# A state-space layer and its FFN on one core: from pairs of units in a loop to one unit a phase, written out

## The reference, cut to what matters

```python
def layer(x, in_proj_w, conv_w, conv_b, x_proj_w, A_log, D, out_proj_w):
    xz = einsum('bld,ed->ble', x, in_proj_w)              # 256 -> 1024
    x_inner, z = split(xz, 2)
    x_conv = silu(causal depthwise conv of x_inner, 4 taps, + conv_b)
    x_dbl = einsum('bld,ed->ble', x_conv, x_proj_w)       # 512 -> 33
    delta, B, C = softplus(x_dbl[..., 0]), x_dbl[..., 1:17], x_dbl[..., 17:]
    A = -exp(A_log)                                       # 16 states
    h = h * exp(delta * A) + x_conv * (delta * B)         # over 2048 steps
    y = (einsum('bdn,bn->bd', h, C) + x_conv * D) * silu(z)
    return einsum('bld,od->blo', y, out_proj_w)           # 512 -> 256
def ffn(x, ...):
    h = butterfly(x @ W_exp + b_exp, up_weights)          # 256 -> 1024
    h = butterfly(gelu(h + up_bias), down_weights)
    return h @ W_con + b_con + down_bias
x = x + layer(layernorm(x), ...)
x = x + ffn(layernorm(x), ...)
```

## Time and profile before

| | |
|---|---|
| median of 3 runs | 630.66 us |
| profiled execution | 632.72 us, span 630.8 us |
| TensorE busy | 560.5 us (89%) |
| VectorE busy | 443.5 us (70%) |
| ScalarE busy | 303.1 us (48%) |
| GpSimd busy | 123.9 us (20%) |
| mean granted TensorE clock | 0.951 |
| instructions in the profile | 8980 |

### The profile page before, as it was taken

One profiled execution on the slowest core, in us unless ns is written; L12 is line 12 of the kernel. 1 busy time (PEld: TensorE's weight loads), 2 busy tenths in 40 slices (PEclk: granted clock), 3 DMA queues, 4 the chain that ended last, 5 costly groups with the idle time before them and its releaser, 6 DMA issues.

```text
span 630.8 us, 8980 instructions
## 1 busy us (share of the span) xinstructions
PE 560.5 (89%) x2996; PEld 436.9 (69%) x2996; DVE 443.5 (70%) x883; ACT 303.1 (48%) x511; POOL 123.9 (20%) x104
## 2 busy tenths in 40 slices
PE   4989776679999997979999989979999988979996
PEld 3747345647899773747899665847899664848895
DVE  5748868876556789877556699887555699977432
ACT  3655739146055766044144866054254865162252
POOL 4213100240012032250021042250020041340010
PEclk9988876899999999979999998979999999979999
DMA  8332020010010100010000000000100000000000
GB/s 239 4 22 4 0 66 2 1 35 2 3 64 2 34 1 2 0 34 0 33 33 0 33 0 0 0 33 0 33 33 0 33 0 0 0 0 2 0 34 34
DMA packets 33067, 12.88 MB, mean 20 GB/s; under 512 B 22003, under 2 KB 32499, under 8 KB 33044
## 3 DMA queue, kind: packets, MB, share of 16 engines
q1 hardware_dynamic: 31444, 9.96, 7.3%
q10 hardware_dynamic: 1600, 2.62, 1.2%
HBM read 8.39 MB, written 4.19 MB: 20 GB/s over the span
## 4 chain that ended last, share of the span: by engine, by line
PE 58%; DVE 23%; ACT 8%; issue 7%; DMA 2%; POOL 1%; DVEq 0%; ACTq 0%; POOLq 0%
PE acc L869 14%; PE wide L858 12%; PE wide L727 8%; DVE xc L1346 6%; PE wide L847 4%; PE wide L829 4%; PE wide L836 4%; PE wide L736 3%; DVE x1b_xn L1255 2%; PE small L717 2%; DVE soft L1385 2%; PE acc L656 1%; PE small L806 1%; DVE diag_sum L1475 1%; PE small L784 1%
## 5 line engine op out<-in xcount | busy, mean ns | idle before, releaser
L1031 ACT ACTIVATE hid_f<-wide,bias_up 128x512 f32<-128x512 f32 x64 | 44.0, 687 | 139.3 <-PE acc L869 127.4
L1346 DVE SCALAR_TENSOR_TENSOR xc<-xi,taps,xc 128x512 f32<-128x512 f32 x96 | 91.0, 958 | 6.5 <-ACT xc L1060 4.2
L1363 DVE TENSOR_TENSOR hid_low<-hid_f,hid_high 128x512 fp32r<-128x512 f32 x64 | 44.3, 692 | 68.8 <-ACT hid_high L1132 68.2
L869 PE MATMUL acc<-w_down_high,hid_high 128*128 128x256 f32 x256 | 73.9, 289 | 1.5 <-DVE hid_low L1363 1.5
L869 PE MATMUL acc<-w_down_low,hid_high 128*128 128x256 f32 x256 | 71.8, 281 | 0.0
L869 PE MATMUL acc<-w_down_high,hid_low 128*128 128x256 f32 x256 | 71.7, 280 | 0.0
L847 PE MATMUL wide<-w_out,yg 128*128 128x256 f32 x256 | 56.9, 380 | 0.0
L537 POOL TENSOR_TENSOR c_place<-xd,row_in_block 128x1024 f32<-128x1024 f32 x8 | 15.5, 1938 | 208.8 <-DVE xd L1374 208.8
L727 PE MATMUL wide<-xnT_high,w_in_high 128*128 128x512 f32 x128 | 54.9, 429 | 0.0
L858 PE MATMUL wide<-xnT_high,w_up_high 128*128 128x512 f32 x128 | 53.4, 417 | 0.0
L869 PEld LDWEIGHTS acc<-w_down_high,hid_high 128*128 128x128 f32 x256 | 48.2, 188 | 6.6 <-DVE hid_low L1363 4.5
(11 more groups left out here) (184 smaller groups left out, 1136.4 us busy)
## 6 DMA issues: line engine op xcount, KB each, us to landing
x_in<-in_L_attn_x_dram SPq DMA_DIRECT2D x8, 512.0 KB, 3.6
out_dram<-x1b_xn SPq DMA_DIRECT2D x8, 512.0 KB, 2.9
xc<-in_L_attn_in_proj_w_dram ACTq DMA_DIRECT2D x2, 512.0 KB, 6.6
xc<-in_L_ffn_W_exp_dram ACTq DMA_DIRECT2D x1, 1024.0 KB, 9.3
low_w<-in_L_ffn_W_con_dram SPq DMA_DIRECT2D x1, 1024.0 KB, 5.6
raw_out<-n_L_attn_out_proj_w_dram ACTq DMA_DIRECT2D x1, 512.0 KB, 10.3
low_w<-in_L_ffn_up_weights_dram SPq DMA_DIRECT2D x14, 4.0 KB
low_w<-_L_ffn_down_weights_dram SPq DMA_DIRECT2D x14, 4.0 KB
```

The lines of the kernel that those rows point to most:

```text
L869: last = pe.matmul(acc[:, c, :], hid[h][:, j % HRING, c * P:(c + 1) * P], w_down[w][:, j, 0:DM], start=j == 0 and c % 2 == 0 and n == 0, s ...
L1031: ins = act.activation(out_ap, in_ap, how.pop("func"), **how)
L1346: ins = dve.scalar_tensor_tensor(xc[b][:, e, :], xi[:, e, tap:tap + TILE], taps[:, e, tap:tap + 1], xc[b][:, e, :], ALU.mult, ALU.add)
L1363: dve.tensor_tensor(hid[1][:, j % HRING, :], hid_f32[:, j % HRING, :], hid[0][:, j % HRING, :].bitcast(F32), ALU.subtract).then_inc(hid_re ...
```

## The change

The loop goes; every engine's program is one sequence of nine phases. Phase u holds the scan of unit u (now numbered 0 to 7, alternating between the sequences), the input projection, convolution and silu of unit u+1, the FFN of unit u-1, and the first norm of unit u+2. With it:

- C is spread by two DMAs through DRAM (`spread_c` on SP: xd out, and back so that each partition has C of its block); `place_c` and the two products go. `diag` has its states innermost, `diagonal_times_c` is one instruction over 1024 elements.
- `x_projection` writes its four products to two halves of the partitions; the sum of the halves is taken in `xd_tokens_first`, now a product with `fold`.
- all four x_tok tiles are copied by ScalarE (two by VectorE before); `silu_z` comes with `silu_x`, behind the gelus of the phase.
- xnT has a buffer for each norm; x is loaded twice (x_ln, x_res); `gate` works in place in xc.
- the FFN weights are finished in phase 1; the DOWN mixing is done at the end of phase 0.
- the instructions that set the semaphores at the start go, and waits before the first use are left out.

```diff
+            def spread_c(u):
+                read(sp, u, "xdtok", 0)
+                wait(sp, c_spread, u, 16, ago=2)
+                sp.dma_start(c_dram[u % BATCH], xd[:, :, 1 + NS:XD]).then_inc(c_out.handle, 16)
+                wait(sp, c_out, u, 16)
+                wait(sp, diag_summed, u, 1, ago=1)
+                sp.dma_start(c_near[:, :, :, :].rearrange("p u c n -> p (u c n)"),
+                             c_dram[u % BATCH].rearrange("(j u) c n -> j (u c n)", u=BL).unsqueeze(1)
+                             .to_broadcast([NB, BL, BL * GR * NS])).then_inc(c_spread.handle, 16)
...
+            for u in range(1, UNITS):                    # SP
+                load_for_residual(u)
+                if u + 2 < UNITS:
+                    load_for_norm(u + 2)
+                spread_c(u)
+                store(u - 1)
...
+            for u in range(UNITS):                       # GpSimd
+                weigh_gaps(u)
+                mask_b(u)
+                diagonal_gaps(u)
+                place_c_block(u)
+                diagonal_times_b(u)
+                if u:
+                    residual_with_bias(u - 1)
+                if u + 2 < UNITS:
+                    rstd_of(u + 2, 0, var1, rstd1)
+                rstd_of(u, 1, var2, rstd2)
...
+                    at = HALF * (g % 2)                  # x_projection
+                    last = pe.matmul(bank[at:at + HALF, :], w_x[:, g, :], xc[u % BATCH][:, g, :], start=g < 2, stop=g >= CB - 2,
+                                     skip_group_check=True)
...
+            def phase(u, beside=..., weights=...):       # TensorE
+                x_projection(u)
+                tokens_first(u)
+                xd_tokens_first(u)
+                beside(6); into(0); into(1); beside(7); into(2); into(3)   # into(e): in_projection(u + 1, e)
+                step_sums(u)
+                beside(8); into(4); decayed_b(u)
+                beside(9); into(5); decayed_c_start(u)
+                beside(10); into(6); decayed_c_block(u)
+                beside(11); into(7); state_inputs(u)
+                beside(12); weights(15); weights(16)
+                ffn(u - 1, 0, 2)
+                off_diagonal(u)
+                beside(13); beside(14)
+                ffn(u - 1, 2, 3)
+                ssm_output(u)
+                ffn(u - 1, 3, 5)
+                out_projection(u, 0)
+                out_projection(u, 1)
+                ffn(u - 1, 5, HB)
+                if u + 2 < UNITS:
+                    transposes(u + 2, "ln1T", x_ln, norm1)
+                ffn(u - 1, HB, HB + 1)
+                transposes(u, "ln2T", xn2, norm2)
+                ffn(u - 1, HB + 1, HB + 2)
...
+            def phase(u, beside=..., scale=..., weights=...):   # ScalarE, v = u + 1
+                take_xd(u)
+                for c in range(GR):
+                    take_x_tok(u, c)
+                load_exp_table()
+                exp_abs(u)
+                place_halo(v); first_tap(v, 0); first_tap(v, 1)
+                first_tap(v, 2); first_tap(v, 3); save_halo(v)
+                exp_sums(u)
+                copy_z(v, 4); exp_gaps(u)
+                copy_z(v, 5); take_c_start(u)
+                exp_diagonal(u)
+                copy_z(v, 6); take_c_block(u)
+                copy_z(v, 7); copy_first_state(u)
+                for n in range(HIGH):
+                    scale(UP, n)
+                weights(15); weights(16)
+                if u:
+                    for j in range(HB):
+                        gelu(u - 1, j)
+                if v:
+                    silu_x(v)
+                    silu_z(v)
+                for n in range(HIGH):
+                    scale(DOWN, n)
+                if u + 2 < UNITS:
+                    high_parts(u + 2, "ln1T")
+                high_parts(u, "ln2T")
...
+            def phase(u, ...):                           # VectorE, v = u + 1; low(j): low_hidden(u - 1, j)
+                take_xd(u); multiply(UP); softplus(u)
+                convolve(v, 0); take_sums(u); convolve(v, 1)
+                weigh(u); weigh_b(u)
+                convolve(v, 2); convolve(v, 3)
+                weights()
+                diagonal_times_c(u); low(0)
+                sum_diagonal(u); assemble(u); advance_state(u)
+                multiply(DOWN); add(UP, 0)
+                low(1); first_stats(u + 2)
+                gate(u, 0); gate(u, 1); low(2)
+                first_normalise(u + 2)
+                gate(u, 2); gate(u, 3)
+                add(UP, 1)
+                low(3)
+                first_residual(u, 0); first_residual(u, 1)
+                second_stats(u)
+                add(UP, 2)
+                low(4); second_normalise(u); low(5)
+                for n in range(HIGH):
+                    add(DOWN, n)
+                low(6)
+                low_parts(u + 2, "ln1T")
+                low(7)
+                low_parts(u, "ln2T")
+                final(u - 1)
```

More of the change, by code:

```diff
@@ L471, in _ @@
[L471 to L473 removed]
+            for u in range(1, UNITS):
[4 more added lines that the diff above has]
+                store(u - 1)
+            store(UNITS - 1)
+            wait(sp, out_stored, UNITS - 1, 16)
         @block.gpsimd
         def _(pool):
[L478 removed]
@@ L762, in step_sums @@
+            def step_sums(u):
+                bank = tile_of("sums", 0, u)
+                free(pe, u, "sums", 0)
+                wait(pe, delta_ready, u, 1)
                 for n, mask in enumerate((upto, block_upto, after)):
@@ L1637, in _ @@
-            second_half(TILES, last=True)
+            dve.wait_ge(early_loaded, 16)
+            wait(dve, norm1, 0, GR)
+            norm_stats(1, 0, x_res, var1, link_setup)
+            written(dve, 0, "ln1T", MB - 1)
+            normalise(1, 0, x_res, x_ln, rstd1, norm1)
+            wait(dve, norm1, 1, GR)
+            constants()
+            for e in range(CB):
+                convolve(0, e)
+            low_parts(1, "ln1T")
+            phase(0, multiply=multiply_paths, add=add_blocks)
```

1154 lines of the change are left out of this document (501 added, 653 removed).

## The result

The changed kernel takes **672.57 us** (median, 671.67 to 672.73) against 630.71 (630.66 before a fourth run was added) on the same chip: a ratio of 1.0656, 95% interval 1.0633 to 1.0678. The forecast was 661 with a range of 640 to 682. The profiled execution has a span of 670.9 us, so the sum of the prediction (659.3) is to be held against that: 11.6 us short.

A forecast was written before the change was run, and what follows sets the result against it. TensorE, busy 93% of a unit, was taken to bound the kernel, with order able to make it wait; 119.5 + 84.3 + 305.2 + 64.5 + 57.7 + 28.1 = 659.3 us of span, plus 1.9: 661 us, range 640 to 682.

The forecast's parts named there:

- The forecast's own case: Whole kernel slower: a phase of 74 to 79, phase 1 starting between 115 and 124, 648 to 675 us; chance 0.60.
- rivals (a) to (d): GpSimd slows nothing, 622 (0.09); no down7 wait, 620 (0.05); projection halves don't overlap, 675 (0.12); low clock lasts, 678 (0.10).
- A phase: Interval between x projections in phases 2 to 5: 76.3 us against 69.7 a unit before.
- The wait behind the silus: Phase's end: down7 waits for low_hidden 7, queued behind gelu 7, silus and norm parts; 9.6 us, TensorE idle 6.8.
- Softplus to the first convolution: VectorE's walk to the gates: 4.5 us, taken from the old kernel; dropping GpSimd's place_c saves nothing.
- The residual add beside the convolutions: GpSimd's add beside VectorE's last convolutions costs 1.5 us, bounds 0 and 2.5.
- The sum over the states: VectorE's product with C and reduction over neighbouring elements: no change, bounds 0.8 us less and 0.5 more.
- The end of phase 0: Setup's end, with VectorE as the chain: phase 1's x projection can start at 119.5 us.
- Phase 1: Phase with the FFN weights in it: 10 us for them, 2 covered, so 76.3 + 8 = 84.3 us.
- Phase 7 and the last FFN: Kernel's end: 57.7 us to phase 7's ln2T and parts, then 28.1 for the last FFN.
- C by DMA: Writing C out and reading it back, costed at nothing: transfers end by 16 us, diagonal_times_c wants it at 27.
- rival (e): C's DMAs late, or straight-line code fetched too slowly; of either size, chance 0.04.

The follow-up runs named there:

- silu_between: Changed kernel with ScalarE's silus of the next unit behind the third gelu of the phase instead of behind the eighth: 636.41 us.
- down7_first: Changed kernel with VectorE's low_hidden(u-1,7) ahead of the low parts of unit u+2's first norm instead of behind them: 672.90 us.
- residual_early: Changed kernel with GpSimd's residual add of the last unit at the head of the phase instead of behind diagonal_times_b: 681.28 us.
- best_order: Changed kernel, only reordered: silus behind gelu 4, block 6 before c_start, low_hidden 7 before low parts, VectorE's last convolution, statistics and normalisation behind the gates: 606.41 us.
- parts_first: Changed kernel with ScalarE's high parts of both norms right behind the last gelu and the silus behind them: 647.51 us.
- best_pool_head: Kernel with silus behind gelu 4 and VectorE's convolution, statistics and normalisation behind the gates, plus GpSimd's residual add at the phase's head: 613.23 us.

## Why the prediction was right, and where its sum was off

The forecast's own case came about, with its mechanism in its place; none of the rivals (a) to (d) did. By its steps, forecast first:

- **A phase**, 76.3: 74.55 to 75.01. The walk to the end of d5 took 62.4 instead of 63.9, the wait 9.3 instead of 9.6, down7 2.86 instead of 2.8. Four phases: 299.2 instead of 305.2, **-6.0**.
- **TensorE's own work**, 61: in silu_between, at full clock, 61.09. The x projection, 1.8: 1.94.
- **The wait behind the silus**: right in cause, and 9.3 us for 9.6 from the end of down5 to down7. TensorE idles 5.2 of these, not 6.8. The text had down7 wait for low_hidden 7; TensorE in fact stops one step before, at the bank for ln2T's second tile, which the same paragraph names, and makes that tile, 1.12 us at the low clock, behind the wait. down7_first showed that the bank is what counts.
- **Softplus to the first convolution**, 4.5: 2.9. "The dropped GpSimd place_c ... saves nothing here" is the sentence that failed. The first instruction of softplus took 1.67 us and takes 0.17 now. I took 1.67 for its length; it was place_c that held it up, which I had looked for beside convolutions only. A small instruction with a long time was the sign. It ended at 366.86, and place_c at 366.84:

```profile
364.89 1.95 POOL L537 TENSOR_TENSOR c_place<-xd,row_in_block 128x1024 f32<-128x1024 f32 x1 [28.05 <-DVE xd L1374]
```

- **The residual add beside the convolutions**, 1.5 with bounds 0 and 2.5: 9.07 - 6.62 = 2.45, the 6.62 being the 4.29 + 2.33 us that these six took in the kernel before; in residual_early they take 7.01. The term was undersized, and the rule of the Trainium skill ("SBUF — State Buffer", Who interferes with whom), that the two instructions exclude each other for a whole one, had given 2.5. With that rule the trace agrees. The row that I went by instead loses less, 1.55 us beside 2.55; why it does is not known.
- **The sum over the states**, no change: the reduction over neighbouring elements takes 1.21 us, mean 1.91 before. It gave 0.7 back. The product with C in one instruction takes 1.22.
- **The end of phase 0**, 119.5: 127.07, **+7.6**. The states end at 79.5, not 77.5; the paths DOWN wait twice for TensorE (6.6 us up to the mixing, not 3.6); the out projection takes 9.96, not 6.9, as the clock is 0.71 there. I had costed a stretch with an idle TensorE by products from a busy one.
- **Phase 1**, 84.3: 89.60, **+5.3**. The weights hold VectorE for 10.8 us, the 10 of the forecast, but none of it is covered; low_hidden 0 waits 2.3 more behind them; the phase begins 1.8 us slower, with the clock at 0.70.
- **Phase 6**, 64.5: 65.24, **+0.7**. **Phase 7 and the last FFN**, 85.8: 89.78, **+4.0**. In phase 7 the weighing of C by its decays took 1.98 us instead of 0.22 beside GpSimd's diagonal_gaps, and the product with C 3.39 instead of 1.22 beside the residual add, at 602.40: 3.9 us of exclusion. The lines are these:

```profile
595.84 1.98 DVE L1382 TENSOR_TENSOR c_block<-xd,decays 128x64 f32<-128x64 f32 x1
...
602.47 3.39 DVE L1419 TENSOR_TENSOR diag<-diag,c_near 128x1024 f32<-128x1024 f32 x1 [3.93 <-POOL diag L588]
```

- **C by DMA**, nothing: no instruction waits for c_spread anywhere in the trace. Nor is any of TensorE's idle time put down to a DMA but the loads at the start, so that neither half of rival (e) shows.

-6.0 + 7.6 + 5.3 + 0.7 + 4.0 = 11.6. Phases 2 to 5 were forecast 2% too high and the four other stretches 5% too low, and the signs partly cancelled: that the total is within 2% is in part luck.

"If order cost nothing, the kernel would gain 8 us or more a unit" stays a bound that no order reached: best_order has 63.5 us a phase, 6.2 less than a unit of the loop, and in all gains 24.7 us, though phases 2 to 6 alone make 32 (four of 6.2 and one of 7.2): phases 0, 1 and 7 with the last FFN take the rest back.

What is open: why the clock falls behind some waits at c_start and not behind others of the same length; and what makes phase 0 come out 2.6 us apart in kernels that have it alike. The clock goes with it: from 30 to 60 us it is 0.83 in the changed kernel and silu_between, whose first states end at 79.5 and 79.3, and 0.77 in parts_first and down7_first, whose states end at 82.6 and 83.2. Why it differs is not known. Nor was the change taken apart further: what C by DMA, the straight-line code and the new place of each copy are worth alone was not measured, only the two halves.

## What to carry to other kernels

When work is moved to the end of a phase, look for who else is queued behind it on that engine: 5.4 us of silus in front of a 0.6 us copy cost 6.8 us a phase, and moved between two gelus they add 0.6 us to TensorE's waits for hid_low and no more. What a saving on the busiest engine is worth depends on the order around it (2.6, 12.3 or 11.2 us for the same edit here), so put the order right first and measure the parts then. Gains of single edits need not add, and an edit can gain where one looks and lose elsewhere: the add at the head of GpSimd's phase gave the convolutions 2 us back and met softplus, at the start of the critical chain.

## What the hardware showed unexpectedly

**GpSimd stops VectorE's small instructions too.** In the kernel before a normalisation of 128x256 took 401 ns at least and 2426 at most, the four of them 5.77 us beside three GpSimd instructions; its VectorE and GpSimd lines:

```profile
412.43 5.77 DVE L1255 TENSOR_SCALAR x1b_xn<-x,mean_var,rstd 128x256 f32<-128x256 f32 x4
```

```profile
412.29 1.98 POOL L555 TENSOR_TENSOR diag<-gaps,rates 128x1024 f32<-128x1024 f32 x1
...
415.34 2.39 POOL L586 TENSOR_TENSOR x1b_xn<-x,bias_out 128x1024 f32<-128x1024 f32 x1
```

In the new order the same four take 1.38 us. One small instruction loses the rest of the GpSimd instruction that runs (1.36, 1.5, 1.8 us were seen): short instructions on the critical chain are the worst place to meet it. Not every one is stopped: in residual_early the copy of xd out of PSUM, at 298.44 and inside the same add, takes 0.29 us, as it does without (0.30). The Trainium skill ("SBUF — State Buffer", Who interferes with whom) says that whoever issues first keeps the shared ports for its whole instruction; the rows agree.

**Equal waits, unequal clocks.** In best_pool_head the wait for c_start was 1.56 to 1.58 us in phases 2 to 6; behind it the clock stayed at 1.0 in two phases and fell in the next three. In the changed kernel the waits were 2.17 to 2.19 us, and the clock stayed in phases 2 to 4 and fell in the other three. In the kernel before, too, the c_start products took 1.09 us behind a wait of 3.00 and 0.63 behind one of 3.01 at 519.21. The length of a wait alone doesn't tell whether the clock falls behind it. Nor is a fall always paid for: it cost 1.5 to 1.8 us a phase in best_pool_head, and 0.1 in the changed kernel's phase 5, where VectorE's chain was longer.
